# First attention of a two-layer transformer: scores and masked squares in blocks of 64 keys on 64x64 tiles, batch loop written out

## The reference

```python
k_C = jnp.einsum('bhk,bhkv->bhv', k_t, C_QV)
G = G + k_t[..., :, None] * k_C[..., None, :]
S_K = S_K + k_t[..., :, None] * k_t[..., None, :]
C_QV = C_QV + q_t[..., :, None] * v_t[..., None, :]
S_C = jnp.einsum('bhkj,bhjv->bhkv', S_K, C_QV)
o_t = jnp.einsum('bhk,bhkv->bhv', q_t, S_C - G)
```

## Time and profile before

| what | us |
|---|---|
| median of 3 runs | 1682.09 (1677.19 to 1685.65) |
| profiled execution, span (its page gives no other time) | 1677.5 |
| first attention, from its first scores to the first scores of its last couple | 122.9 to 789.0 |
| one batch of it in the loop | 42.4 |
| PE busy over the span | 1552.2 |
| VectorE busy over the span | 904.4 |

### The profile page before, as it was taken

How to read it: one execution, slowest core, us unless ns; L and a number is a source line. 1 busy time by engine, 2 the same in 40 slices (tenths; PEclk the granted TensorE clock), 3 DMA queues, 4 the chain that set the end, 5 groups by cost and what they waited for, 6 DMA issues and landing times. The chain is left out here.

```text
span 1677.5 us, 38807 instructions
## 1 busy us (share of the span) xinstructions
PE 1552.2 (93%) x14424; PEld 1233.4 (74%) x14424; DVE 904.4 (54%) x3193; ACT 732.4 (44%) x1975; POOL 299.0 (18%) x376
## 2 busy tenths in 40 slices
PE   6899999999999999999599999959999999999996
PEld 5668888888888888888365656537777777777764
DVE  5336545454545454545322222237877777777774
ACT  2322222222222222222223232258888888888873
POOL 2010201111111101010430000003323332333232
PEclk9999999999999999999699999979999999999998
DMA  4009400000000000000243232258889998899886
GB/s 118 0 8 86 105 8 7 8 8 6 6 6 5 7 5 7 3 10 4 85 114 114 77 112 85 72 166 245 250 241 251 237 250 235 246 246 254 236 235 173
DMA packets 234032, 181.50 MB, mean 108 GB/s; under 512 B 82703, under 2 KB 223913, under 8 KB 233888
## 3 DMA queue, kind: packets, MB, share of 16 engines
q1 hardware_dynamic: 228514, 167.17, 37.1%
q0 software_dynamic: 5376, 12.44, 2.7%
HBM read 103.63 MB, written 75.78 MB: 107 GB/s over the span
## 5 line engine op out<-in xcount | busy, mean ns | idle before, releaser
L1547 ACT ACTIVATE a1Pm<-a1Pm,a1nmx 128x256 f32<-128x256 f32 x512 | 255.5, 504 | 0.4 <-DVE a1nmx L1609 0.3
L1609 DVE CUSTOM_DVE_ANT_0 a1Pm<-a1ps_S,a1Sb 128x256 f32<-128x256 f32 x512 | 196.1, 421 | 77.2 <-issue 75.5
L768 DVE TENSOR_TENSOR a0AT<-a0ps_AM,mask 128x384 f32<-128x384 f32 x256 | 125.5, 551 | 192.5 <-PE a0ps_AM L588 192.1
L773 DVE TENSOR_TENSOR a0MT<-a0ps_AM,mask 128x384 f32<-128x384 f32 x256 | 138.4, 555 | 88.2 <-PE a0ps_AM L609 85.1
L1542 ACT ACTIVATE a1Rt<-a1ps_R 128x384 f32<-128x384 f32 x264 | 128.6, 487 | 106.7 <-PE a1ps_R L1407 96.9
L1162 DVE TENSOR_TENSOR f1hid<-f1ge,f1ps_b 128x512 f32<-128x512 f32 x80 | 55.0, 688 | 192.1 <-PE f1ps_b L1095 182.4
L1426 PE MATMUL a1ps_T<-ident,a1Pm 128*128 128x128 f32 x1024 | 155.9, 275 | 0.0
L607 PE MATMUL a0ps_AM<-a0AT 128*128 128x256 f32 x512 | 152.9, 380 | 0.0
L572 PE MATMUL a0ps_qk<-xnT_all,a0w_in 128*128 (+1 forms) x512 | 138.3, 393 | 2.0 <-PEq L151 1.3
L715 ACT ACTIVATE a0qk<-a0ps_qk 128x512 f32<-128x512 f32 x128 | 76.4, 597 | 119.3 <-PE a0ps_qk L572 119.3
L1407 PE MATMUL a1ps_R<-rel_st,a1stk 72*128 72x192 bf16 x528 | 90.0, 253 | 35.5 <-ACT a1Rt L1542 13.2
(11 more groups left out here) (246 smaller groups left out, 2991.0 us busy)
## 6 DMA issues: line engine op xcount, KB each, us to landing
skew<-a1Rt SPq DMA_DIRECT2D x132, 384.0 KB, 5.4
a1Sb<-skew SPq DMA_DIRECT2D x131, 384.0 KB, 7.0
a1stk<-parts SPq DMA_DIRECT2D x153, 64.0 KB
a1stk<-parts SPq DMA_DIRECT2D x51, 192.0 KB
parts<-a1prt SPq DMA_DIRECT2D x18, 384.0 KB
f1w<-in_L_ffn_w_kernel SPq DMA_DIRECT2D x16, 344.0 KB
f1w<-in_L_ffn_w_kernel SPq DMA_DIRECT2D x16, 320.0 KB
f1wo<-in_L_ffn_wo_kernel SPq DMA_DIRECT2D x16, 320.0 KB
```

The source lines that it names most:

```text
L768: nc.vector.tensor_tensor(AT[i][h][:, :], ps_AM[i][h][:, 0:HB], mask[:, :], ALU.mult).then_inc(A_ready, 1)
L773: nc.vector.tensor_tensor(MT[i][h][:, :], ps_AM[i][h][:, 0:HB], mask[:, :], ALU.mult).then_inc(M_ready, 1)
L1547: nc.scalar.activation(Pm[:, place(h), :], Pm[:, place(h), :], ACT.Exp, bias=nmx[it][:, h:h + 1], scale=-1.0, accum_out=den[it][:, h:h + 1 ...
L1609: nc.vector.tensor_tensor_reduce(out=Pm[:, place(h), :], in0=ps_S[hp % 2][:, n, :], in1=bias_of(it, hp, n), scale=-1.0, scalar=3.0e38, op0 ...
```

## The change

Scores are now computed in blocks of 64 keys (j = 0 to 3). Block j has the queries from j x 64 on, so 256, 192, 128 and 64 columns. Each is a matmul of 64 rows by 64 columns of the array: the row half is the head's, the column half follows from `side`: for pair 0, head h goes to half h, for pair 1 to the other one. The blocks of both heads of a pair lie in one bank, in the two partition halves; blocks 0 and 2 go to bank `ps_AM[i][0]`, 1 and 3 to `ps_AM[i][1]`. VectorE masks two heads at a time with `mask_A`, a constant that GpSimd makes in `front_stage`, 384 and 256 columns wide.

Squares are built from these blocks, 64 x 64 output rows at a time: output block q of a head is the sum over j up to q of the products of blocks, in the partition half q mod 2. Squares are masked as before; two corners of PSUM that no matmul writes are cleared once by VectorE, and TensorE waits for that (`cleared`).

TensorE's scores of a couple wait for both pairs' projections and for all four masked squares of the couple before. The projection of the next couple's second pair moves ahead of `values`, and on ScalarE its copy ahead of the values' copy. The loop over batches is written out on all three engines.

```diff
+NJ = T // DK
+JBANKS = ((0, 2), (1, 3))
+SBANK = [sum(T - j * DK for j in js) for js in JBANKS]
+SCOL = {0: 0, 2: T, 1: SBANK[0], 3: SBANK[0] + T - DK}
...
+                nc.gpsimd.memset(mask_A[:, :], 1.0).then_inc(cs, 1)
+                pool.wait_ge(cs, 19)
+                for j in range(NJ):
+                    for h in range(2):
+                        rows = slice(h * DK, (h + 1) * DK)
+                        nc.gpsimd.tensor_copy(mask_A[rows, SCOL[j]:SCOL[j] + DK], mask[rows, h * DK:(h + 1) * DK]).then_inc(cs, 1)
...
-        AT = [[m.sb(f"a0AT{i}{h}", [P, HB]) for h in range(2)] for i in range(2)]
+        AT = [m.sb(f"a0AT{i}", [P, SBANK[0] + SBANK[1]]) for i in range(2)]
...
+        def side(i, h):
+
+            h = h if i == 0 else 1 - h
+            return slice(h * DK, (h + 1) * DK)
+
         def groups(eng, batch):
...
-            pair(0)
-            pair(1)
-            with eng.Fori(2, NG - 1) as G:
+            for G in range(NG):
                 pair(G)
-            pair(NG - 1)
...
-                def scores(b, p):
-                    i, n = p % 2, b * PAIRS + p
-                    pe.wait_ge(qk_ready, n + 1)
-                    if later(b, p):
-
-                        pe.wait_ge(M_ready, n * 2 - 2)
-                    for h in range(2):
-                        r = slice(h * DK, (h + 1) * DK)
-                        nc.tensor.matmul(ps_AM[i][h][:, 0:T], qk[i][r, 1, 0:P], qk[i][r, 0, :], start=True, stop=True)
-                        nc.tensor.matmul(ps_AM[i][h][:, T:HB], qk[i][r, 1, P:T], qk[i][r, 0, P:T],
-                                         start=True, stop=True).then_inc(A_done, 1)
+                def scores(b, u):
+
+                    pe.wait_ge(qk_ready, b * PAIRS + 2 * u + 2)
+                    if u > 0 or not isinstance(b, int) or b > 0:
+                        pe.wait_ge(M_ready, (b * COUPLES + u) * 4)
+                    for k, js in enumerate(JBANKS):
+                        for j in js:
+                            c = SCOL[j] - k * SBANK[0]
+                            for i in range(2):
+                                for h in range(2):
+                                    r = slice(h * DK, (h + 1) * DK)
+                                    ins = nc.tensor.matmul(ps_AM[i][k][side(i, h), c:c + T - j * DK], qk[i][r, 1, j * DK:(j + 1) * DK],
+                                                           qk[i][r, 0, j * DK:T], start=True, stop=True)
+                                if j == js[-1]:
+                                    ins.then_inc(A_done, 1)
...
-                def squares(b, p):
-                    i = p % 2
-                    for h in range(2):
-                        pe.wait_ge(A_ready, (b * PAIRS + p) * 2 + h + 1)
-                        S, M = AT[i][h], ps_AM[i][h]
-                        nc.tensor.matmul(M[:, 0:T], S[:, 0:P], S[:, 0:T], start=True, stop=True)
-                        nc.tensor.matmul(M[:, T:HB], S[:, P:T], S[:, P:T], start=True, stop=False)
-                        nc.tensor.matmul(M[:, T:HB], S[:, T:HB], S[:, T:HB], start=False, stop=True).then_inc(M_done, 1)
+                def square(i, h, q, j):
+
+                    c, n = SCOL[j] + (q - j) * DK, T - q * DK
+                    rows, to = slice(q % 2 * DK, (q % 2 + 1) * DK), q // 2 * P + q * DK
+                    return nc.tensor.matmul(ps_AM[i][h][rows, to:to + n], AT[i][side(i, h), c:c + DK], AT[i][side(i, h), c:c + n],
+                                            start=(j == 0), stop=(j == q))
+
+                def squares(b, u, i):
+
+                    pe.wait_ge(A_ready, (b * COUPLES + u) * 4 + 3 + i)
+                    for turn in (((0, 0), (1, 0)), ((1, 1),), ((2, 0),), ((2, 1), (3, 0)), ((3, 1),), ((2, 2), (3, 2)), ((3, 3),)):
+                        for h in range(2):
+                            for q, j in turn:
+                                ins = square(i, h, q, j)
+                            if (q, j) == (NJ - 1, NJ - 1):
+                                ins.then_inc(M_done, 1)
...
-                        scores(b, p)
-                        scores(b, p + 1)
+                        scores(b, u)
...
-                        squares(b, p)
-                        squares(b, p + 1)
+                        squares(b, u, 0)
+                        squares(b, u, 1)
...
-                        values(b, u, bb)
-                        if behind and u == 0:
-                            project_out(b - 1)
                         if u < COUPLES - 1:
                             project_qk(b, p + 3)
                         elif more:
                             project_qk(b + 1, 1)
+                        values(b, u, bb)
+                        if behind and u == 0:
+                            project_out(b - 1)
...
                 pe.wait_ge(loaded, 16 * 4)
+                pe.wait_ge(cleared, 1)
...
-                        keep_v(c)
                         if u < COUPLES - 1 or more:
                             keep_qk(n + 3, 1)
+                        keep_v(c)
...
+                def mask_scores(c):
+                    for k in range(2):
+                        cols = slice(k * SBANK[0], k * SBANK[0] + SBANK[k])
+                        for i in range(2):
+                            v.wait_ge(A_done, c * 4 + k * 2 + i + 1)
+                            nc.vector.tensor_tensor(AT[i][:, cols], ps_AM[i][k][:, 0:SBANK[k]], mask_A[:, cols], ALU.mult).then_inc(A_ready, 1)
...
+                for i in range(2):
+                    ins = nc.vector.memset(ps_AM[i][1][DK:P, SBANK[1]:SBANK[1] + DK], 0.0)
+                ins.then_inc(cleared, 1)
```

More of the change, by code:

```diff
@@ L95, with front_stage @@
 BIG = 3.0e38
-def front_stage(nc, a, x_all, xnT_all, ident, mask, iota_e, ltri, ones_bf, group_base, one, router, attn_load, attn_loaded, load_tables):
+def front_stage(nc, a, x_all, xnT_all, ident, mask, mask_A, iota_e, ltri, ones_bf, group_base, one, router, attn_load, attn_loaded, load_tables):
     XL = 4
@@ L201, in _ @@
                                         base=0, pattern=[[1, P]], channel_multiplier=-1).then_inc(cs, 1)
-                pool.wait_ge(cs, 18)
+                nc.gpsimd.memset(mask_A[:, :], 1.0).then_inc(cs, 1)
[4 more added lines that the diff above has]
+                        nc.gpsimd.tensor_copy(mask_A[rows, SCOL[j]:SCOL[j] + DK], mask[rows, h * DK:(h + 1) * DK]).then_inc(cs, 1)
+                pool.wait_ge(cs, 19 + 2 * NJ)
             @block.vector
@@ L401, in _, with attn0_stage @@
                     outputs(g)
-def attn0_stage(nc, a, x_all, xnT_all, xn_all, w_in, w_out, loaded, mask, one, zeros, ident, router, iota_e, ltri, ones_bf,
+def attn0_stage(nc, a, x_all, xnT_all, xn_all, w_in, w_out, loaded, mask, mask_A, one, zeros, ident, router, iota_e, ltri, ones_bf,
                 group_base, gates, slot_ids, send_ids, sent, tin, front, bias_q, bias_k, bias_v, rel_st, tabs, pick, fold):
@@ L462, in attn0_stage @@
         ps_p = [ps_g[:, T + (k + 1) * TPG * E:T + (k + 2) * TPG * E].rearrange("p (q e) -> p q e", q=TPG) for k in range(2)]
-        zero_ready, zeroed = m.sem("a0zero_ready"), m.sem("a0zeroed")
+        zero_ready, zeroed, cleared = m.sem("a0zero_ready"), m.sem("a0zeroed"), m.sem("a0cleared")
         xb_ready = m.sem("a0xb_ready")
@@ L574, in project_qk @@
                     ins.then_inc(qk_done, 1)
-                def later(b, p):
-                    return p > 1 or not isinstance(b, int) or b > 0
-                def scores(b, p):
-                    i, n = p % 2, b * PAIRS + p
-                    pe.wait_ge(qk_ready, n + 1)
-                    if later(b, p):
-                        pe.wait_ge(M_ready, n * 2 - 2)
-                    for h in range(2):
-                        r = slice(h * DK, (h + 1) * DK)
-                        nc.tensor.matmul(ps_AM[i][h][:, 0:T], qk[i][r, 1, 0:P], qk[i][r, 0, :], start=True, stop=True)
-                        nc.tensor.matmul(ps_AM[i][h][:, T:HB], qk[i][r, 1, P:T], qk[i][r, 0, P:T],
-                                         start=True, stop=True).then_inc(A_done, 1)
+                def scores(b, u):
[12 more added lines that the diff above has]
+                                    ins.then_inc(A_done, 1)
                 def values(b, u, bb):
@@ L764, in _ @@
             def _(v):
-                def mask_A(n, i):
-                    for h in range(2):
-                        v.wait_ge(A_done, n * 2 + h + 1)
-                        nc.vector.tensor_tensor(AT[i][h][:, :], ps_AM[i][h][:, 0:HB], mask[:, :], ALU.mult).then_inc(A_ready, 1)
+                def mask_scores(c):
[4 more added lines that the diff above has]
+                            nc.vector.tensor_tensor(AT[i][:, cols], ps_AM[i][k][:, 0:SBANK[k]], mask_A[:, cols], ALU.mult).then_inc(A_ready, 1)
                 def mask_M(n, i):
@@ L909, in batch @@
                     for u in range(COUPLES):
-                        for i in range(2):
```

(7 more changed lines are left out.)

## The result

The changed kernel takes 1589.65 us (median of 4 runs, 1587.17 to 1592.76) where the kernel before took 1679.64 beside it: ratio 0.9468, 95% interval 0.9441 to 0.9495. A second measurement gave 0.9465 (0.9433 to 0.9497). Forecast were 1592 us and a range of 1570 to 1632. The two profiled executions are 1677.5 and 1591.2 us long.

A forecast was written before the change was run, and what follows sets the result against it. The stage was taken as bound by TensorE's stream. 85 (couples) + 4 (loop) + 3 (batch 1) - 1.4 (third couples) - 0.3 (additions) = 90 us less, 1592 us from a median of 1682.1; range 1570 to 1632.

The forecast's parts named there:

- The couple: Scores and squares of two pairs (four heads): 1.33 us less net, 9.40 to 8.07, times 64 makes 85 us less.
- 0.35 of switches: Tile-shape changes around squares between full-array projections: 0.15 us on the way in, 0.20 on the way out.
- Four at once: Scores and squares on four 64x64 tiles running together: 1.10 + 2.19 us a couple, against 2.20 + 4.39 two at once.
- Both doubts: That scores and squares (rival A), or scores alone (Rival B), go only two tiles at a time.
- rival A: Array serves 64x64 tiles two at a time in scores and squares: slower, 1802 us; chance 0.07.
- Rival B: Two row halves can't write one PSUM bank, so scores go two at a time: 70 us lost, 1662; chance 0.07.
- The loop: Batch loop written out: ten batches at 0.4 us, 4 us less; bounds 4 us lost and 10 gained.
- Batch 1: Normalisation comes before 184 us, ahead of GpSimd's table step, so PE's stall shrinks: 0 to 5 us less, 3 taken.
- The third couple: Where experts are chosen too, masks end at 8.19 us: PE waits about 0.2 us in 7 batches, 1.4 in all.
- The additions at the start: GpSimd's new mask hidden; VectorE clearing two corners ahead of the first projection costs 0 to 1.1 us, 0.3 taken.
- Rival C: Something a little late each time, issue limit (22 us) or a lost 0.1 us cover (6 us): 1600 to 1632; chance 0.15.
- The thin cover of the second projection's copy: With that projection ahead of values, its copy is covered by 0.1 us; 0.2 us late would cost 6 us.

The follow-up runs named there:

- the loop's experiment: The kernel before with only its batch loop written out; ratio 0.9969, 5 us less.
- the last two merged kernels: Changed kernel, squares straight after outputs, both projections together behind them: values sharing the first projection's PSUM bank, ratio 0.9451; sharing the outputs' bank, 0.9413.
- the two-tile experiment: Changed kernel without the swap of column halves, so a couple's scores fall on two 64x64 tiles instead of four; 1672 us, ratio 0.9918.
- the run in plain order: Changed kernel with a pair's squares issued head by head and block by block instead of in turns over the tiles; ratio 1.0229.
- the three slower variants of the changed kernel: Changed kernel with scores on two tiles (ratio 0.9918), squares in plain order (1.0229), or values ahead of the second projection again (0.9772).
- the last experiment: Merged-projection kernel with values in the outputs' bank, plus VectorE's table work behind masked squares and the cleared-corner wait ahead of first scores; 1577.88 us, ratio 0.9385.
- run 80: Not a follow-up run: "run" is a verb here, squares run 80 passes in 2.39 us.
- two others with the same loop: The kernel before with GpSimd's second table step held back to the first normalisation (ratio 1.002) or to the third couple's masked squares (0.9961).

## Why the prediction was right

*The couple.* Forecast 1.33 us less for each. Against the straight code of the loop's experiment, an even and an odd batch together go from 41.72 + 42.19 to 36.51 + 36.83 us, which is 1.32 a couple; over 63 steps 83 us. Scores came out at the 1.25 worked out. For the squares, which stand between two full-array projections, I had 2.19 us of stream and 0.35 of switches; projection, squares, projection and values take 5.40 us (651.04 to 656.44) where they took 6.33 in the earlier trace rows, so the squares with their switches went from 3.51 to 2.58: 0.39 of switches. That the price lies in drain and first load is shown by the last two merged kernels.

*Four at once.* Both doubts fell to the row of four passes in 0.45 us. Under rival A the scores of the changed kernel would look like those of the two-tile experiment. The rule of the Trainium skill ("TensorE: Matmul & The Clock Gate", Part 3), that matmuls start in program order, does not hold here: in the run in plain order head 1's first pass begins ahead of four passes of head 0 that the code issues earlier. That run also shows what is right in it: the reach is short. Rival B needed row halves that can't share a bank; here heads 0 and 1 of a pair wrote one bank in different partition halves at full rate. The Trainium skill, "TensorEngine Tiling (Array Packing)", Gotcha 1, rules that out, and the measurement decides against it for such halves. Two row halves in the same half of a bank were not tried.

*The loop.* 4 us forecast, 4.4 in the trace, of which 2.0 are the turns of the one profile; the timed 5 us has an interval of 2 to 8.

*Batch 1.* 3 us forecast, 3.8 measured: the whole stall is 5.06, and 1.25 stayed (37.75 against the 36.51 of such a batch). The normalisation now comes ahead of the step, as forecast and as the timelines of VectorE and GpSimd show beside the earlier trace rows:

```profile
184.85 0.60 DVE L827 TENSOR_SCALAR n1xn<-x_all,n1mean,n1rstd 128x128 f32<-128x128 f32 x2
185.37 0.60 DVE L831 TENSOR_SCALAR xn_all<-x_all,n1mean,n1rstd 128x128 f32<-128x128 f32 x2
```

```profile
187.95 8.87 POOL L555 TENSOR_TENSOR t1rvd<-t1rv 1x4088 f32<-1x4088 f32 x1 [58.33 <-DMA rv_table<-t1rvd]
```

But part of that is luck. The normalisation came 4.5 us earlier (184.85 against 189.34), not some 8 and not before 184 us, and the step, which hangs on a DMA, began 3.0 us later (187.95 against 184.98). At its old time it would have met the normalisation. The margin is thin: in the three slower variants of the changed kernel the normalisation came after the step's start, and this couple took 16.99, 12.84 and 17.03 us. Why the step moved is not shown.

The 1.25 us that stayed belong to a term that the prediction left out. ScalarE loads a table once in this stage, ahead of the root that this first normalisation waits for; the masks behind it end late, and PE waits:

```profile
183.12 1.28 ACT L748 ACT_TABLE_LOAD   x1
...
187.97 1.32 PE L599 MATMUL a0ps_AM<-a0qk 64*64 64x256 f32 x32 [1.16 <-DVE a0MT L796]
```

The prediction's own sum for such a couple, 7.94 us, with these 1.28 makes 9.22 against its 8.07: a wait of 1.15.

*The third couple.* The wait of 0.2 us, 1.4 us in all, did not come: there are no PE waits between 269.9 and 636.7 us. In such a couple, begun at 619.71, the masks ended at 625.95 + 1.94 = 627.89 us, 8.18 us in, where 8.19 were forecast. But the next scores began at 628.03, 0.1 us behind them, as the ranks of the routing make that couple 8.32 us long, 0.2 more than a clean one, which I had left out. The two rows:

```profile
625.95 1.94 DVE L796 TENSOR_TENSOR a0MT<-a0ps_AM,mask 128x384 f32<-128x384 f32 x4
```

```profile
628.03 1.32 PE L599 MATMUL a0ps_AM<-a0qk 64*64 64x256 f32 x32
```

*Two more terms were mis-sized.* The additions at the start cost 1.1 us, not 0.3: the first projection waits for the cleared corners (0.4 us), and the scores for both projections' copies at once, where they used to wait for one. And 64 couples was too many: two in batch 0 did not get their 1.33 us. In the first, an instruction of VectorE's table work stands beside GpSimd's first step. It stood before the change too, until the same moment, so the four masks behind it end at 132.8 us in both kernels; but the scores of before needed only the first two of them, and those of now need all four. PE waits 2.16 us where it waited 1.09 (first the rows of before):

```profile
125.86 3.83 DVE L883 TENSOR_SCALAR t1rpad<-t1rk 8x129 f32<-8x129 f32 x1
...
132.02 0.71 PE L587 MATMUL a0ps_AM<-a0qk 64*128 64x256 f32 x4 [1.09 <-DVE a0MT L773]
```

```profile
126.70 3.00 DVE L906 TENSOR_SCALAR t1rpad<-t1rk 8x129 f32<-8x129 f32 x1
```

```profile
132.96 1.40 PE L599 MATMUL a0ps_AM<-a0qk 64*64 64x256 f32 x32 [2.16 <-DVE a0MT L796]
```

After that wait the granted clock was 0.64 over 4.15 us, where it was 1.00 before the change (stretches, columns as in the earlier trace rows, first that of before):

```profile
132.00:137.00 5.00, 4.98 (x42) 4.11 (x43) 4.45 (x10) 1.17 (x2) 0.00 (x0) 1.00 0.82 90
```

```profile
132.90:137.05 4.15, 4.09 (x49) 2.85 (x49) 3.08 (x8) 0.00 (x0) 0.00 (x0) 0.64 0.83 79
```

Outputs took 2.76 us there instead of 1.45, a good part at 1.2 GHz. Wait and clock are 2.5 us: the first couple got 0.2 us shorter and the second 0.1 longer, where each was to lose 1.33. Without the wait, in the last experiment, the second takes a clean couple's time (7.91 us). The prediction looked for stalls in batch 1 only.

The sum for the stage: 83.2 + 4.4 + 3.8 - 2.5 = 88.9 us; measured 666.05 - 577.32 = 88.7. With 1.1 lost ahead of it and 1.3 behind it the span fell by 86.3. The forecast of 90 was the sum of a very good main term and small ones whose errors partly cancel; that the timed medians differ by 90.0 us is closer than these terms deserve.

*Rival C.* The 31.6 ns of the earlier trace rows are no limit of issue: squares run 80 passes in 2.39 us, 30 ns each with their switches, which is what the columns and the switches ask for, and the last eight passes of a couple's scores, 64 columns wide on four tiles, all start within 0.08 us (from 649.365 us on). The thin cover of the second projection's copy held.

## What to carry to other kernels

Where TensorE's stream is the bound, price it in columns and passes for each tile of the array, add the drain and first load for each change of shape (0.20 us to visit the full array here), and issue tiles in turns: a pass goes past only a few waiting ones. Before merging two visits, look for who shares a PSUM bank with the moved work; a copy 0.08 us late took back most of the gain. Look for long GpSimd instructions beside VectorE work that PE waits for; a kernel that gets faster or slower elsewhere slides in and out of them, and that alone moved these times by up to 8 us. And look for who waits behind the first use of a function on ScalarE: here it brought a table load of 1.28 us.

## What had not been expected of the hardware

- A VectorE instruction of 128 columns with one input, from SBUF to SBUF, stands until a GpSimd step ends: 9.10 us for two of 0.3. Masks out of PSUM beside the same step kept their 1.95 us for four, and one of a single column its 0.14.
- A wait of 2.16 us on PE was followed by a granted clock of 0.64 over 4.15 us; the same place after a wait of 1.09 us kept 1.00.
- In the couple looked at, a pass goes past at most five earlier ones that have not begun; head 1 idled on a free row half for 1 us because its passes stood further back.
- The turns of the loop cost 0.3 to 0.45 us in one profiled kernel and nothing in two others with the same loop.
